# GpSimd's split of a bias, moved behind two batches and cut in three, with new static orders (one core, fused four-layer kernel)

## The reference

```python
# layer 0 ffn (the first stage), per batch b
n1 = layernorm(x0)                       # LN0, RA0, NH0: statistics, 1/sqrt, normalise
rw = gating(n1, smha_sim, smha_gates)    # LOG0, GA0, RG0, GB0, GX0, GE0
q, k, v = sum over 8 experts of rw[e] * n1 @ proj[e]
hs = x0 + sum_e rw[e] * (softmax(q k') v) @ o_proj[e]
n2 = layernorm(hs); rw2 = gating(n2, ...)
hs + sum_e rw2[e] * gelu(n2 @ w1[e]) @ w2[e]
# layer 1 cond: up, gate, silu, down with one chosen expert per batch; then 16 gate logits
# layer 2 ffn: logits = x @ phi_w + phi_b     <- phi_b is "the slot bias", 2048 numbers
# layer 3 cond: per batch b, sum over e of (weight[e] * mask) * cond_8[b, e]
```

## Time and profile before

| | us |
|---|---|
| median of 3 runs | 1338.59 |
| the profiled execution | 1348.07 |
| its span | 1346.3 |
| TensorE busy | 1107.3 (82%) |
| VectorE busy | 749.8 (56%) |
| ScalarE busy | 448.1 (33%) |
| GpSimd busy | 176.7 (13%) |

### The profile page before, as it was taken

One profiled execution on the slowest core, in us unless ns is written; L12 is line 12 of the kernel. 1 busy time (PEld: TensorE's weight loads), 2 busy tenths in 40 slices (PEclk: granted clock), 3 DMA queues, 4 the chain that ended last, 5 costly groups with the idle time before them and its releaser, 6 DMA issues.

```text
span 1346.3 us, 17637 instructions
## 1 busy us (share of the span) xinstructions
PE 1107.3 (82%) x6726; PEld 784.2 (58%) x6726; DVE 749.8 (56%) x1645; ACT 448.1 (33%) x712; POOL 176.7 (13%) x170
## 2 busy tenths in 40 slices
...
DMA packets 12890, 35.21 MB, mean 26 GB/s; under 512 B 3552, under 2 KB 7296, under 8 KB 12035
## 3 DMA queue, kind: packets, MB, share of 16 engines
...
...
## 4 chain that ended last, share of the span: by engine, by line
PE 56%; issue 16%; DVE 13%; POOLq 4%; DVEq 4%; ACT 3%; POOL 2%; SPq 1%; DMA 1%; ACTq 0%
PE ps L1079 5%; PE ps L983 4%; PE ps L1009 4%; PE ps L1213 3%; PE ps L961 3%; PE ps L798 3%; PE ps L954 3%; PE ps L946 3%; PE ps L1067 3%; PE ps L808 2%; PE ps L1140 2%; DVE arena L1867 2%; PE ps L1156 2%; PE ps L844 2%; PE ps L832 1%
## 5 line engine op out<-in xcount | busy, mean ns | idle before, releaser
L1867 DVE TENSOR_REDUCE arena<-ps 128x8 f32<-128x2048 f32 x32 | 73.2, 2288 | 31.9 <-PE ps L1120 31.7
L1418 ACT ACTIVATE arena<-ps 128x2048 f32<-128x2048 f32 x32 | 60.1, 1879 | 84.0 <-PE ps L1144 84.0
L983 PE MATMUL ps<-arena,uR 128*128 128x512 f32 x128 | 76.8, 684 | 4.7 <-ACT arena L1364 4.7
L1009 PE MATMUL ps<-arena 128*128 128x128 f32 x512 | 70.9, 296 | 11.8 <-DVE xacc L1789 8.1
L1009 PEld LDWEIGHTS ps<-arena 128*128 128x128 f32 x512 | 66.1, 208 | 19.0 <-DVE xacc L1789 10.7
L1067 PE MATMUL ps<-uR,arena 128*128 128x256 f32 x256 | 74.5, 387 | 0.7 <-ACT arena L1391 0.7
L1079 PE MATMUL ps<-arena 128*128 128x256 f32 x256 | 63.5, 397 | 5.2 <-DVE arena L1848 3.7
L1213 PE MATMUL ps<-arena 128*128 128x512 f32 x128 | 62.4, 632 | 3.4 <-DVE yT L1934 2.0
L1391 ACT ACTIVATE arena<-ps 128x512 f32<-128x512 f32 x64 | 38.3, 598 | 75.5 <-PE ps L1068 66.5
L798 PE MATMUL ps<-arena 128*128 128x256 f32 x256 | 59.7, 392 | 2.6 <-DVE arena L1616 2.6
L954 PE MATMUL ps<-x2R,arena 128*128 128x256 f32 x192 | 54.0, 404 | 9.3 <-DVE arena L1757 9.1
...
## 6 DMA issues: line engine op xcount, KB each, us to landing
...
```

The source lines that it names most:

```text
L983: mm(o, uR[:, b, k * P:(k + 1) * P], phiC[:, col:col + 512], start=True, stop=False)
L1009: last = mm(high[:, 2, t * P:(t + 1) * P], eD[h][:, k, col:col + P], uT[u][:, k, :], start=k == 0, stop=k == 1)
L1418: av(pexp[:, t, gp].rearrange("p c h t -> p (c h t)"), scores[:, :, :].rearrange("p c t -> p (c t)"), ACT.Exp, scale=SCALE3).then_inc(s.sc ...
L1867: V.tensor_reduce(nm[:, k, :, 2 * gp:2 * gp + 2], scores[:, :, :].rearrange("p c (h t) -> p c h t", h=2), X, ALU.max, negate=True).then_in ...
```

## The change

`PH` is cut into three entries, `PHA` (the cast), `PHB` (the multiplication) and `PHC` (the subtraction), and a drain is put ahead of the cast. In GpSimd's order they no longer stand first, but behind `RG0.1`, with `RA` and `RG` entries between them; `PX.0` and the `W` entries stand later too. The strings of PE, ACT and DVE of the first stage are new. No computation is added or removed; SP's string and the second stage's orders are unchanged.

```diff
     "PE": """
-    COND.0 NT0.0 LOG0.0 GTR0.0 SPR0.0 COND.1 QK.0 NT0.1 VT.0 SC.0 LOG0.1 PT.0 AT.0 GTR0.1 SPR0.1 O1.0 COND.2
-    QK.1 NT1.0 NT0.2 VT.1 SC.1 LOG1.0 MH0.0 PT.1 MH1.0 LOG0.2 AT.1 GTR1.0 SPR1.0 O1.1 MOE.0 GTR0.2 NT1.1 UG0.0
-    COND.3 LOG1.1 SPR0.2 UG1.0 NT0.3 MH0.1 LOG0.3 DN.0 QK.2 L1G.0 MH1.1 SC.2 GTR1.1 VT.2 SPR1.1 PT.2 GTR0.3 AT.2
-    COND.4 MOE.1 SPR0.3 UG0.1 O1.2 UG1.1 QK.3 DN.1 NT1.2 SC.3 L1G.1 NT0.4 LOG1.2 VT.3 PT.3 MH0.2 GTR1.2 MH1.2
+    COND.0 NT0.0 LOG0.0 GTR0.0 SPR0.0 COND.1 QK.0 NT0.1 VT.0 LOG0.1 SC.0 PT.0 AT.0 GTR0.1 SPR0.1 COND.2 O1.0
+    QK.1 NT1.0 VT.1 SC.1 LOG1.0 NT0.2 MH0.0 PT.1 MH1.0 LOG0.2 AT.1 GTR1.0 SPR1.0 O1.1 MOE.0 GTR0.2 NT1.1 UG0.0
+    SPR0.2 LOG1.1 COND.3 UG1.0 MH0.1 DN.0 MH1.1 QK.2 L1G.0 GTR1.1 NT0.3 SC.2 SPR1.1 LOG0.3 VT.2 PT.2 MOE.1 AT.2
+    GTR0.3 UG0.1 COND.4 SPR0.3 O1.2 UG1.1 NT0.4 QK.3 LOG0.4 DN.1 NT1.2 SC.3 L1G.1 LOG1.2 VT.3 PT.3 GTR0.4 MH0.2
...
     "DVE": """
-    LN0.0 NH0.0 GA0.0 GB0.0 GE0.0 LN0.1 S8A0.0 S8A1.0 NH0.1 MXA.0 GA0.1 GB0.1 S8B0.0 GE0.1 S8B1.0 S8A0.1 S8A1.1
-    LN1.0 LN0.2 NH1.0 NH0.2 MXA.1 GA1.0 GB1.0 GA0.2 S8B0.1 GE1.0 S8B1.1 GB0.2 S8M0.0 S8M1.0 GE0.2 LN1.1 NH1.1
-    X1.0 LN0.3 GA1.1 HM0.0 NH0.3 GB1.1 S8A0.2 HM1.0 S8A1.2 GE1.1 GA0.3 GB0.3 GE0.3 LA.0 L1.0 MXA.2 S8M0.1 S8M1.1
+    LN0.0 NH0.0 GA0.0 GB0.0 GE0.0 LN0.1 S8A0.0 S8A1.0 NH0.1 GA0.1 MXA.0 GB0.1 GE0.1 S8B0.0 S8B1.0 LN0.2 S8A0.1
+    S8A1.1 LN1.0 NH0.2 NH1.0 MXA.1 GA1.0 GB1.0 GA0.2 S8B0.1 GE1.0 S8B1.1 GB0.2 S8M0.0 S8M1.0 GE0.2 LN1.1 NH1.1
+    X1.0 HM0.0 GA1.1 LN0.3 S8A0.2 HM1.0 S8A1.2 GB1.1 NH0.3 GE1.1 LA.0 MXA.2 L1.0 GA0.3 S8M0.1 S8M1.1 GB0.3 GE0.3
...
     "POOL": """
-    PH.0 RA0.0 PH.1 PX.0 RG0.0 PH.2 PH.3 W.0 WA.0 RA0.1 W.1 WA.1 W.2 WA.2 W.3 WA.3 RG0.1 W.4 WA.4 W.5 WA.5 W.6
-    RA1.0 WA.6 RA0.2 W.7 WA.7 RG1.0 RG0.2 RA1.1 RA0.3 RG1.1 RG0.3 RA0.4 RA1.2 RG1.2 RG0.4 RA1.3 RA0.5 RG1.3
...
+    RA0.0 RG0.0 RA0.1 RG0.1 PHA.0 PHB.0 PHC.0 PHA.1 PHB.1 RA0.2 PHC.1 RA1.0 PHA.2 PHB.2 PHC.2 PHA.3 PHB.3 RG1.0
+    PHC.3 W.0 RG0.2 WA.0 PX.0 W.1 RA1.1 WA.1 W.2 WA.2 RA0.3 RG1.1 W.3 WA.3 W.4 WA.4 W.5 WA.5 W.6 RG0.3 WA.6 W.7
+    WA.7 RA0.4 RA1.2 RG0.4 RG1.2 RA1.3 RA0.5 RG1.3 RG0.5 RA0.6 RA1.4 RG1.4 RG0.6 RA1.5 RA0.7 RG1.5 RG0.7 RA1.6
...
-                if n == "PH":
-                    half = slice(HALF * (b // 2), HALF * (b // 2) + HALF)
+                half = slice(HALF * (b // 2), HALF * (b // 2) + HALF)
+                if n == "PHA":
                     if b == 0:
                         pool.wait_ge(s.consts_bf, 1)
                         pool.wait_ge(s.b_loaded, 16 * len(b_loads))
+                    pool.drain()
                     G.tensor_copy(phib_h, phib[:, half])
+                if n == "PHB":
                     pool.drain()
                     G.tensor_scalar(phib_t, phib_h, cpart[0:3, b % 2:b % 2 + 1], None, ALU.mult)
+                if n == "PHC":
                     pool.drain()
                     G.tensor_tensor(phib[:, half], phib[:, half], phib_t, ALU.subtract)
                     pool.drain()
```

More of the change, by code:

```diff
@@ L113 @@
     "PE": """
-    COND.0 NT0.0 LOG0.0 GTR0.0 SPR0.0 COND.1 QK.0 NT0.1 VT.0 SC.0 LOG0.1 PT.0 AT.0 GTR0.1 SPR0.1 O1.0 COND.2
-    QK.1 NT1.0 NT0.2 VT.1 SC.1 LOG1.0 MH0.0 PT.1 MH1.0 LOG0.2 AT.1 GTR1.0 SPR1.0 O1.1 MOE.0 GTR0.2 NT1.1 UG0.0
-    COND.3 LOG1.1 SPR0.2 UG1.0 NT0.3 MH0.1 LOG0.3 DN.0 QK.2 L1G.0 MH1.1 SC.2 GTR1.1 VT.2 SPR1.1 PT.2 GTR0.3 AT.2
-    COND.4 MOE.1 SPR0.3 UG0.1 O1.2 UG1.1 QK.3 DN.1 NT1.2 SC.3 L1G.1 NT0.4 LOG1.2 VT.3 PT.3 MH0.2 GTR1.2 MH1.2
-    AT.3 LOG0.4 SPR1.2 O1.3 MOE.2 GTR0.4 NT1.3 UG0.2 COND.5 SPR0.4 LOG1.3 UG1.2 MH0.3 MH1.3 QK.4 DN.2 GTR1.3
@@ L119 @@
[L119 to L123, removed]
@@ L124 @@
-    "ACT": """
[L125 to L129, removed]
@@ new lines @@
+    SPR0.2 LOG1.1 COND.3 UG1.0 MH0.1 DN.0 MH1.1 QK.2 L1G.0 GTR1.1 NT0.3 SC.2 SPR1.1 LOG0.3 VT.2 PT.2 MOE.1 AT.2
+    GTR0.3 UG0.1 COND.4 SPR0.3 O1.2 UG1.1 NT0.4 QK.3 LOG0.4 DN.1 NT1.2 SC.3 L1G.1 LOG1.2 VT.3 PT.3 GTR0.4 MH0.2
+    AT.3 MH1.2 GTR1.2 COND.5 SPR1.2 O1.3 MOE.2 SPR0.4 NT1.3 UG0.2 LOG1.3 NT0.5 UG1.2 MH0.3 LOG0.5 QK.4 DN.2
+    GTR1.3 MH1.3 L1G.2 GTR0.5 SC.4 VT.4 SPR1.3 PT.4 COND.6 AT.4 MOE.3 SPR0.5 UG0.3 O1.4 UG1.3 QK.5 DN.3 NT1.4
+    SC.5 L1G.3 NT0.6 LOG1.4 VT.5 LOG0.6 PT.5 MH0.4 GTR1.4 MH1.4 AT.5 SPR1.4 O1.5 MOE.4 GTR0.6 NT1.5 UG0.4 COND.7
```

26 lines of the change are left out of this document (22 added, 4 removed).

## The result

The changed kernel takes 1329.76 us (median of 6 runs, 1329.49 to 1331.24), the kernel before 1338.7 (6 runs, 1337.62 to 1346.53): a ratio of 0.9921, 95% interval 0.9895 to 0.9947. It is faster, by 8.9 us between the medians and not by 26. The interval allows 7 to 14 us: the kernel before scatters, and over its 62 executions in all rounds beside the profiled ones (1337.1 to 1348.4 us) the median is 1341.3 and not 1338.7. The profiled execution is an ordinary one, 1329.5 us, span 1327.7; against the profiled one before (1348.07) that is 18.6 us.

A forecast was written before the change was run, and what follows sets the result against it. The head of GpSimd's queue was taken as the bound; 30.2 - 1.6 - 2.5 - 1 + 1 = 26.1 us of gain, taken whole off the median 1338.59 us, gave 1312.5 us, range 1304 to 1325.

The forecast's parts named there:

- What bounds the kernel: First stage ahead of 107 us: the head of GpSimd's queue, where PH.0 held the powers, is the bound.
- Steps 1 to 4: Batches 0 and 1: RA0.0, RG0.0, RA0.1, RG0.1 go ahead of PH, PX, W entries; 30.2 us gained together.
- step 4: Batch 1's first gating: RG0.1 ahead of all W; transpose at 65.7 instead of 95.91 us, 11 us gained.
- Step 5: GpSimd's postponed PH, PX, W, WA delay NH1.1 (1.6 us), RG0.3 (2.5), GB1.0 and GE1.0 (1).
- rival B: The postponed GpSimd work holds four gatings, 16 us on the path: gain 14, time 1324.5 us; chance 0.17.
- Step 6: New strings for batches 2 to 7: +1 us, bounds -5 and +8.
- From the profile to the median: Gain from the profiled execution (1348.07 us) taken whole off the median 1338.59 us, giving 1312.5 us.
- PHB by the rule of the Trainium skill: GB0.1 and GE0.1 beside PHB.0 would by the rule lose up to 2.3 us, gain 24.
- B's sign: First stage's end above 361 us, against 349 us forecast, would show the postponed GpSimd work taking the gain back.
- A: Postponed work hides fully and the strings close small waits from 105 us on: gain 35, time 1303.5 us; chance 0.14.
- C's sign: Several-us gaps each batch ahead of attention or mixture would show them chained: 10 us slower, 1348.5 us; chance 0.04.
- D: Powers come early, but something else, such as weights, holds QK.0 or QK.1: time 1338 us; chance 0.03.

The follow-up runs named there:

- e3: Only GpSimd's order from the changed kernel; PE, ACT and DVE strings and the powers' sequence as in the kernel before: 1338.5 us, ratio 0.9957.
- e1: Changed kernel with all PH, PX, W and WA behind the last RG of GpSimd's order; first stage ends at 345.4 us, no total given.
- e9: Changed kernel with each W and WA issued as four instructions of 256 columns instead of one of 1024: 1330.6 us.
- b3: The kernel before, unchanged, profiled again for one of its shorter executions: 1337.9 us, first stage ends at 368.3 us.
- e7: Only the new strings of PE, ACT and DVE, with GpSimd's old placement (PH first): 1348.0 us, ratio 1.0043.
- e2: Old strings of PE, ACT and DVE, GpSimd's powers in old sequence, all PH, PX, W, WA last; stage ends at 345.2 us, no total given.

## Why the prediction was wrong

1. *What bounds the kernel*: right. The head of GpSimd's queue held the chain, and taking it away brought `QK.1` 31.6 us forward, and nearly as far with the old strings (e3, 75.5). (That GpSimd's work lies nearly all in 33 to 101 us holds for the first stage only: 60.0 of its 94.2 us there; 82.6 us more lie behind the stage.)
2. *Steps 1 to 4 (30.2 us)*: right in the mechanism, and in the sum by some luck. The first power ends at 28.8 us, the transpose of `GTR0.1` starts at 64.9 (forecast 65.7), the backlog at 58.3 (forecast 61). Nor was `QK.0` held by weights. But two errors cancel in step 4: `GB0.1` started at 59.1 us and not at 62.1, since `QK.0` came at 43.9 and took 8.7 us instead of 10; and the gating took 5.8 us and not 3.6, since `PHC.0` held the last instruction of `GE0.1` (2.35 us instead of 0.23).
3. *Step 5, what the backlog holds up (5.1 us)*: this is the step that failed. It is 15.1 us (e1 against the changed kernel). In the terms of the sum, 31.6 us were won up to `QK.1` and 17.4 lost from there to the stage's end (269.7 us before, 287.1 after), where steps 5 and 6 together had 4.1 of loss. Of the 17.4 us 15.6 are idle time of TensorE; its busy time is the old one but for 1.8, as forecast. `NH1.1` was priced rightly (2.63 us instead of 0.60; TensorE waits 1.31 us for it). "`GB1.0` and `GE1.0` beside `PHC.3` and `W.0`: ... I take 1 us, bounds 0 and 4" was 6.05 us on TensorE's wait (8.42 against 2.37 in e1): four instructions were held, 6.5 us in all, not two, and `RG1.0` was 1.9 us late behind `PHB.3`. The gating of batch 1's second gate (`GE1.1`), which now lies beside `W.3` to `WA.5`, I did not price at all in the sum: 9.8 us held, 5.29 on TensorE's wait. And the 2.5 us for `RG0.3` was for a lateness that came only in e9; in the changed kernel its input came late too (it ran at 141.0 us, GpSimd having stood idle for 3.42). The backlog ended at 148.8 us, not near 140. I had the row for this price (2.15 against 0.17) and used it for rival B, as four gatings of 4 us.
4. *Step 6, the strings (+1, bounds -5 and +8)*: their worth depends on GpSimd's order: some -5 with the old one, 0 without a backlog, +8 with the new one (e7, e1 and e2, e3). I treated it as one number that adds up.
5. *From the profile to the median*: "the gain lies in waits, not in the rest, so I take it whole" failed too. The 9.5 us by which the profiled execution was longer lay, by b3, two thirds within the first stage and one third behind it, and the change doesn't keep them. With step 5 right (gain 14) the sum would have given 1324.5 us; the other 5.3 us are this point.
6. *PHB by the rule of the Trainium skill* (GPSIMD Engine Reference, "Key points"): by the rule as written the gating beside `PHB.0` would be held; I went by the row. After, `GB0.1` ran beside `PHB.0` (59.46 to 62.31) with its small instructions at 0.16 to 0.18 us but for one of 0.75 at 59.83, and was held only by `PHC.0`. The row was right.
7. *Rivals*: B was the mechanism, and the stage's gain is its 14 us. The number is in part luck: B has four gatings on the path, and TensorE waited at two of them (8.42 and 5.29 us; 0 at `GTR0.2`, 0.61 at `GTR0.3`). The stage's end, 360.6, lies 0.4 us below the 361 that I had set as B's sign. A is shut out by e1 and e2: with no backlog beside it the stage ends 29.3 us earlier than before, not 35; C's sign would be a wait ahead of L824 or L856 in each batch, and in TensorE's list of waits from 60 us on none of these is above 0.8 us; D is shut out by point 2.
